# Gated cross-attention and two mixture-of-experts stages: the second stage's shared experts woven into the cross-attention, and ring numbers read at another place

## The chip, the cores and the metric

One NeuronCore of a Trainium2 chip runs the whole program in one launch. The metric is the device time in microseconds. Three runs of the kernel before gave 1206.42, 1208.92 and 1210.02 us; their median, 1208.92 us, is the time before. One more execution was profiled: it took 1207.77 us, of which the instructions span 1205.9 us.

## What is computed

2048 tokens (4 batches of 512) of 256 numbers go through four residual steps.

```python
x = x + tanh(g_xattn[0]) * windowed_attention(layernorm(x), ctx)       # 16 heads, window 64
x = x + tanh(g_ffn[0])   * moe0(layernorm(x))   # 32 experts of 128, top 8 in 4 of 8 groups, 1 shared expert of 128
x = x + tanh(g_xattn[1]) * bidaf(layernorm(x), ctx)
x = x + tanh(g_ffn[1])   * moe1(layernorm(x))   # 8 experts of 256, top 2 by softmax + bias, shared experts of 512 hidden

# bidaf, per batch (hc = normalised x, hq = ctx)
Sim = (hc@w1)[:,:,None] + (hq@w2)[:,None,:] + einsum('bid,bjd->bij', hc*w3, hq) + b
hq_hat = softmax(Sim, 2) @ hq
hc_bar = softmax(max(Sim, 2), 1) @ hc
out = concat([hc, hq_hat, hc*hq_hat, hc*hc_bar]) @ W_qv + b_qv
# moe1
scores = softmax(xt @ gate_w.T); idx = top_k(scores + gate_bias, 2); w = scores[idx]
y = sum_e w_e * (silu(xt@w1[e].T) * (xt@w3[e].T)) @ w2[e].T
z = silu(xt@sw1.T) * (xt@sw3.T) @ sw2.T
moe1 = y + z
```

## The kernel before

Five engines run programs written out by hand and meet at semaphores: TensorE (`pe`, shown as PE), ScalarE (`act`), VectorE (`dve`), GpSimd (`pool`) and SyncE (`sp`), which issues most loads. The residual `x` stays in on-chip memory as 16 tiles of 128 tokens. The order of work on each engine is the order of its code; nothing is scheduled automatically.

The program has five parts. First the windowed attention. Then the front of expert stage 0 (logits, routing, shared expert) and its sparse part: every (token, expert) choice has a slot, slots are cut into blocks of 128 that belong to one expert each, 159 blocks. Then the cross-attention, one iteration per batch (`tensor_a1`, `scalar_a1`, `vector_a1`). Then the front of expert stage 1 (`moe_tensor` and its fellows with `L == 1`) and its sparse part, 39 blocks, each with two halves of the expert's 256 hidden numbers. At the end the rows are gathered back and added.

The front of stage 1 treats the shared experts as 4 units of 128 hidden numbers and goes over unit and batch, v = 0 to 15. Inputs, weights and hidden values are split into a high and a low fp32r part (`xh`, `xl`, `wh`, `wl`, `hidh`, `hidl`), and each product is made of three: `gate_up` has 12 products of 512 columns per v, `down` 12 of 256 columns. The logits are 8 products of 512 columns per batch, turned by token afterwards. VectorE does the routing between those units: `first`, softmax, sort, mark, `ranked`, one-hot tables (`hots`, two buffers), index lists (`indices`).

In the cross-attention an iteration has on TensorE: `transposes` of the normalised input, `scores` (four products pairs into two banks, each waiting for VectorE's maximum and ScalarE's exp), `probs_transposed`, `attended`, `context_bar`, `output`. VectorE adds the gathered rows of stage 0 for the next batch in the middle of it (`y_pair_added`), takes the residual of the last batch, and normalises.

In the sparse parts (`sparse_tensor`) a step k has: `slots_transposed` of block i+2, `gate_up(k)`, `hidden_transposed(k - 1)`, `down(k - 2)`. The expert's weights lie in a ring of four, and the ring number of block i is read by TensorE's queue from a table in memory (`value_load`) at the head of the block, ahead of everything else of it; in stage 1 a second number is read there, the count of loads that must have landed.

## Time and profile before

| | us |
|---|---|
| median of three runs | 1208.92 |
| profiled execution | 1207.77 |
| its span | 1205.9 |
| PE busy | 919.2 (76%) |
| DVE busy | 733.9 (61%) |
| POOL busy | 531.6 (44%) |
| ACT busy | 442.2 (37%) |

By the trace the stretches are: sparse part of stage 0 from 377 to 658 us, cross-attention from 717.7 us (its second, third and fourth iteration begin at 763.1, 809.0 and 854.5, and the last product ends at 899.2), front of stage 1 until 1010.4, its sparse part until 1154, and the gathering of rows until the end. Matmuls overlap in the records: of a chain of products, the time from one start to the next tells more than the duration. A plain fp32 product appears as two records, an fp32r product or a transposition as one.

### The profile page before, as it was taken

Reading aid. Unit: us, or ns where it says so; the run is one execution under the profiler, and the core shown is the slowest. Engines: PE = TensorE matmul, PEld = TensorE weight load, DVE = VectorE, ACT = ScalarE, POOL = GpSimd, SP = SyncE. Lnnn points to the kernel's source line nnn. Section 1 sums busy time; section 2 is a strip of 40 time slices with the busy share of each in tenths; the row PEclk is TensorE's granted clock in tenths of the full one; section 3 lists DMA queues with packets and bytes.
Section 4 is the critical chain, followed back from the end, with each engine's and each line's share of the span. In section 5 each row is a group of like instructions: output and inputs, shape, how many; then the busy total and the mean of one; then the engine's idle time right before and its main releaser. Section 6 shows DMA issues by size and latency. Waiting matters only on the chain. (4 is left out here: it accounts for less than half of the span.)

```text
span 1205.9 us, 20553 instructions
## 1 busy us (share of the span) xinstructions
PE 919.2 (76%) x5501; PEld 693.9 (58%) x5501; DVE 733.9 (61%) x2093; ACT 442.2 (37%) x1048; POOL 531.6 (44%) x584
## 2 busy tenths in 40 slices
PE   3478888865577999999998019889898968999920
PEld 3467777753334777777776005455566856677610
DVE  6769999996654865555554255787744765433322
ACT  5559888943132333333333002202214241222200
POOL 7246656542004655555551777786002204222045
PEclk9679999988656999999999558987999989999965
DMA  8930000022002676666666534333014001335234
GB/s 248 216 72 2 0 0 0 1 67 70 1 0 66 210 208 193 201 205 206 186 170 128 196 98 128 113 105 88 1 42 133 2 1 57 102 86 152 83 101 130
DMA packets 65690, 122.62 MB, mean 102 GB/s; under 512 B 10497, under 2 KB 41474, under 8 KB 65474
## 3 DMA queue, kind: packets, MB, share of 16 engines
q0 software_dynamic: 17184, 46.95, 15.1%
q1 hardware_dynamic: 21474, 48.62, 13.8%
q10 hardware_dynamic: 26944, 25.96, 6.2%
q8 instruction: 45, 0.74, 0.2%
q14 instruction: 43, 0.35, 0.1%
HBM read 80.33 MB, written 32.24 MB: 93 GB/s over the span
## 5 line engine op out<-in xcount | busy, mean ns | idle before, releaser
L1278 POOL DMA_INDIRECT xg<-token_rows,gather_idx x198 | 188.1, 950 | 278.9 <-PE bank L944 182.7
L955 PE MATMUL bank<-sw,xgt 128*128 x948 | 255.0, 392 | 1.0 <-DVE shid L1208 0.9
L1294 POOL DMA_INDIRECT yg<-slot_rows,slot_of x160 | 170.1, 1063 | 111.7 <-DMA slot_rows<-ysb 63.5
L955 PEld LDWEIGHTS bank<-sw,xgt 128*128 128x128 f32 x948 | 166.2, 192 | 22.7 <-issue 2.6
L1075 ACT ACTIVATE ssil<-bank 128x128 f32<-128x128 f32 x237 | 65.7, 277 | 243.3 <-PE bank L955 243.3
L970 PE MATMUL bank<-sw,sht 128*128 x474 | 141.8, 381 | 0.0
L1202 DVE COPY xgt<-bank 128x256 f32<-128x256 f32 x198 | 83.8, 424 | 93.4 <-PE bank L944 91.1
L1215 DVE COPY sht<-bank 128x128 f32<-128x128 f32 x237 | 69.1, 292 | 117.3 <-PE bank L963 117.0
L548 ACT ACTIVATE prob<-bank,nmax 128x256 f32<-128x256 f32 x256 | 111.4, 510 | 7.1 <-DVE nmax L612 7.1
L1309 DVE SCALAR_TENSOR_TENSOR x<-yg,gate_of,x 128x256 f32<-128x256 f32 x160 | 65.8, 479 | 78.3 <-DMA yg<-slot_rows,slot_of 78.3
L430 PE MATMUL bank<-consts,prob 128*128 128x128 f32 x512 | 84.0, 289 | 33.5 <-DVE ptl L620 31.2
L612 DVE TENSOR_REDUCE nmax<-bank 128x2 f32<-128x512 f32 x128 | 87.7, 686 | 17.6 <-PE bank L417 17.1
L1082 ACT ACTIVATE ysb<-bank 128x256 f32<-128x256 f32 x198 | 75.9, 383 | 54.3 <-PE bank L970 54.3
L944 PE MATMUL bank<-consts,xg 128*128 128x128 f32 x396 | 79.1, 283 | 21.0 <-issue 10.1
L538 ACT ACTIVATE pth<-bank 128x512 f16<-128x512 f32 x128 | 80.0, 625 | 33.8 <-PE bank L430 33.5
L620 DVE TENSOR_TENSOR ptl<-bank,pth 128x512 f16<-128x512 f32 x128 | 87.2, 681 | 0.9 <-ACT pth L538 0.8
L944 PEld LDWEIGHTS bank<-consts,xg 128*128 128x128 f32 x396 | 48.1, 142 | 66.2 <-issue 51.4
L430 PEld LDWEIGHTS bank<-consts,prob 128*128 128x128 f32 x512 | 57.9, 146 | 48.5 <-ACT prob L548 26.7
L970 PEld LDWEIGHTS bank<-sw,sht 128*128 128x128 f32 x474 | 71.6, 191 | 18.1 <-issue 0.6
L417 PE MATMUL bank<-kst,qm 128*128 (+1 forms) x256 | 78.7, 391 | 0.0
L664 POOL TENSOR_TENSOR qm<-qst,consts 128x512 fp32r<-128x512 f32 x64 | 67.6, 1086 | 21.5 <-ACT qst L480 21.5
L881 PE MATMUL bank<-hot_hi,hot_tok 128*128 128x159 f16 (+1 forms) x160 | 43.6, 427 | 35.0 <-ACT hot_tok L1035 34.5
(211 smaller groups left out, 1688.1 us busy)
## 6 DMA issues: line engine op xcount, KB each, us to landing
slot_rows<-ysb ACTq DMA_DIRECT2D x98, 256.0 KB, 3.1
sw<-in_w SPq DMA_DIRECT2D x48, 384.0 KB
kst<-khl SPq DMA_DIRECT2D x32, 224.0 KB, 5.4
token_rows<-xn SPq DMA_DIRECT2D x8, 512.0 KB, 4.9
xg<-token_rows,gather_idx POOLq DMA_INDIRECT x198, 3.3
yg<-slot_rows,slot_of POOLq DMA_INDIRECT x160, 2.8
x<-in_x SPq DMA_DIRECT2D x4, 512.0 KB, 5.7
craw<-in_ctxt SPq DMA_DIRECT2D x4, 512.0 KB, 6.5
```

The costliest lines, as they stand in the source:

```text
L417: mm = pe.matmul(sp[:, hh * WIN:(hh + 1) * WIN], qm[:, par, hh, k, :], ks, start=False, stop=True, skip_group_check=True)
L430: mm = pe.transpose(bank[2 + (k + 1) % 2][:, hh * WIN + kb * P:hh * WIN + kb * P + P], prob[:, (k + 1) % 4, hh, kb * P:(kb + 1) * P], ident)
L538: nc.scalar.activation(pth[:, (k + 1) % 4], bank[2 + (k + 1) % 2][:, :].rearrange("p (a b) -> p a b", a=2), ACT.Copy).then_inc(s_pth, 1)
L548: e = nc.scalar.activation(prob[:, k % 4, hh, :], s_bank(k, par)[:, hh * WIN:(hh + 1) * WIN], ACT.Exp, bias=nmax[:, k % 4, hh:hh + 1])
L612: nc.vector.tensor_reduce(nmax[:, k % 4, :], s_bank(k, par)[:, :].rearrange("p (a b) -> p a b", a=2), AX_X, ALU.max, negate=True).then_inc ...
L620: nc.vector.tensor_tensor(ptl[:, k % 4], bank[2 + k % 2][:, :].rearrange("p (a b) -> p a b", a=2), pth[:, k % 4], ALU.subtract).then_inc(s ...
L944: mm = pe.transpose(bank[i % 2][:, c * P:(c + 1) * P], xg[:, (first + i) % XG_RING, c * P:(c + 1) * P], ident)
L955: mm = pe.matmul(bank[2 + k % 2][:, 0:2 * FF], xgt[:, i % 3, c * P:(c + 1) * P], w[:, :, c, :], start=(c == 0), stop=(c == CH - 1))
L970: pe.matmul(bank[6 + i % 2][:, 0:DIM], sht[:, k % 2, :], sw[:, bass.ds(slot[i] + u, 1), 2 * CH * FF:WCOLS], start=(u == 0), stop=(u == hal ...
L1202: nc.vector.tensor_copy(xgt[:, i % 3, :], bank[i % 2][:, 0:CH * P]).then_inc(s_xtl, 1)
L1278: nc.gpsimd.indirect_dma_start(xg[:, (first + i) % XG_RING, 0:ROW[L]], None, rows[L], bass.IndirectOffsetOnAxis(gather_idx[:, i:i + 1], 0) ...
L1294: nc.gpsimd.indirect_dma_start(yg[:, t % Y_TILES, j, :], None, ybuf[L], bass.IndirectOffsetOnAxis(slot_of[:, t, j:j + 1], 0)).then_inc(s_y ...
```

## The change

The front of stage 1 is taken apart. Its logits and shared experts are computed in plain fp32 instead of in three fp32r products, from one buffer of the turned input (`xt1`), one of all shared weights (`wsh1`) and one of hidden values (`hid1`), and they are put into the cross-attention: in iteration b the work of batch b-1 (and the down products of b-2). What is left after the last iteration is the work of the last batch and the routing. VectorE's row terms now come behind the four maxima, and the normalising of batch b-1 is done in one piece ahead of them. The one-hot tables have four buffers instead of two in both stages. TensorE reads the ring numbers of block i+1 behind the gate products of block i instead of at the head of block i+1.

```diff
+HOTS = 4
-                if t >= 2:
-                    dve.wait_ge(m.hotf, m.n["hotf"] + t - 1)
+                if t >= HOTS:
+                    dve.wait_ge(m.hotf, m.n["hotf"] + t - HOTS + 1)
...
+            def block_numbers(i):
+                slot[i] = pe.value_load(wslot[0:1, i:i + 1], min_val=0, max_val=W_RING - halves)
+                if L == 1:
+                    loads[i] = pe.value_load(needed[0:1, i:i + 1], min_val=16, max_val=16 * (E0 + 2 * E1))
+            block_numbers(0)
             slots_transposed(0)
             slots_transposed(1)
             for k in range(blocks * halves):
                 i = k // halves
                 if k % halves == 0:
-                    slot[i] = pe.value_load(wslot[0:1, i:i + 1], min_val=0, max_val=W_RING - halves)
                     if L == 1:
-                        pe.wait_ge(s_sw, pe.value_load(needed[0:1, i:i + 1], min_val=16, max_val=16 * (E0 + 2 * E1)))
+                        pe.wait_ge(s_sw, loads[i])
                     if i + 2 < blocks:
                         slots_transposed(i + 2)
                 gate_up(k)
+                if k % halves == 0 and i + 1 < blocks:
+                    block_numbers(i + 1)
                 if k >= 1:
                     hidden_transposed(k - 1)
...
+            def logits(b):
+                pe.wait_ge(m.xh, n1["xh"] + 2 * b + 2)
+                for j in range(TPB):
+                    for c in range(CH):
+                        mm = pe.matmul(bank[3][:, j * E1:(j + 1) * E1], xt1[:, c, j * P:(j + 1) * P], rraw[:, c, 0:E1],
+                                       start=(c == 0), stop=(c == CH - 1))
+                mm.then_inc(m.lg, 1)
+            def shared_gate_up(b, u):
+                v = SH1 * b + u
+                if v == 0:
+                    pe.wait_ge(m.wload, 16)
+                else:
+                    pe.wait_ge(m.h, n1["h"] + v)
+                if u == 0:
+                    pe.wait_ge(A["p"], 4 * min(b + 2, BATCH))
+                for half, ready in ((0, m.gate), (1, m.up)):
+                    for c in range(CH):
+                        w = slice((CH * half + c) * FF, (CH * half + c + 1) * FF)
+                        mm = pe.matmul(bank[half][:, :], wsh1[:, u, w], xt1[:, c, :], start=(c == 0), stop=(c == CH - 1))
+                    mm.then_inc(ready, 1)
...
             for b in range(BATCH):
                 transposes(b)
+                if b >= 2:
+                    shared_down(b - 2)
                 scores(b)
+                if b:
+                    inputs_turned(b - 1)
+                    logits(b - 1)
+                    shared_gate_up(b - 1, 0)
                 probs_transposed(b)
                 maxima_transposed(b)
                 attended(b)
+                if b:
+                    shared_gate_up(b - 1, 1)
                 context_bar(b)
+                if b:
+                    shared_gate_up(b - 1, 2)
+                output(b, (0,))
+                if b:
+                    shared_gate_up(b - 1, 3)
+                output(b, (2,))
+            b = BATCH - 1
+            shared_down(b - 1)
+            inputs_turned(b)
+            logits(b)
+            shared_gate_up(b, 0)
+            shared_gate_up(b, 1)
+            ranks(pe, 1, m)
+            shared_gate_up(b, 2)
+            table(pe, 1, m, range(0, 8))
+            shared_gate_up(b, 3)
+            table(pe, 1, m, range(8, TILES))
+            expert_row(pe, 1, m)
+            shared_down(b)
...
+            def shared_silu(b, u):
+                act.wait_ge(m.gate, m.n["gate"] + SH1 * b + u + 1)
+                if b:
+                    act.wait_ge(m.y, m.n["y"] + b)
+                nc.scalar.activation(hid1[:, u, :], bank[0][:, :], ACT.Silu).then_inc(m.sil, 1)
...
+                if b == 1:
+                    sp.dma_start(wsh1[:, :, :], w1_in[0:SH1].rearrange("u p c -> p u c")).then_inc(m.wload, 16)
+                if b >= 2:
+                    rows_stored(sp, 1, m, b - 2)
```

TensorE in the sparse part of stage 1, one block. L982 and L984 read the ring number and the load count, L944 transposes slots, L955 is gate and up, L963 turns the hidden values, L970 is down; ISA rows work out addresses. Before:

```order
L982 TENSOR_LOAD wslot
L982 ISA x2
L984 TENSOR_LOAD needed
L984 ISA x2
L944 MATMUL bank<-consts,xg 128x128 x2
L955 ISA
L955 MATMUL bank<-sw,xgt 128x256
L955 ISA
L955 MATMUL bank<-sw,xgt 128x256
L963 MATMUL bank<-consts,shid 128x128
```

The same block after, where L930 is the transposition of slots, L941 gate and up, L966 and L968 the reads, L949 the turning of hidden values, L956 down:

```order
L930 MATMUL bank<-consts,xg 128x128 x2
L941 ISA
L941 MATMUL bank<-sw,xgt 128x256
L941 ISA
L941 MATMUL bank<-sw,xgt 128x256
L966 TENSOR_LOAD wslot
L966 ISA x2
L968 TENSOR_LOAD needed
L968 ISA x2
L949 MATMUL bank<-consts,shid 128x128
L956 ISA
L956 MATMUL bank<-sw,sht 128x256
```

The reads have moved from ahead of the slots' transposition to between the gate and up products and the turning of hidden values.

TensorE in the third iteration of the cross-attention, from its first transposition to the attended product, before (L1589 `transposes`, L1600 `scores`, L1612 `probs_transposed`, L1633 `attended`):

```order
L1589 MATMUL bank<-consts,xn 128x128 x8
L1600 MATMUL bank<-craw,aenc 128x512 x8
L1612 MATMUL bank<-consts,prob 128x128 x16
L1618 MATMUL bank<-consts,mx 1x128
L1633 MATMUL bank<-p1t,traw 128x512 x4
```

And after (L1627 `shared_down`, L1590 `inputs_turned`, L1601 `logits`, L1617 `shared_gate_up`):

```order
L1503 MATMUL bank<-consts,xn 128x128 x8
L1627 MATMUL bank<-wsh,hid 128x256 x16
L1516 MATMUL bank<-craw,aenc 128x512 x8
L1590 MATMUL bank<-consts,xn 128x128 x8
L1601 MATMUL bank<-rraw,xt 128x8 x8
L1617 MATMUL bank<-xt,wsh 128x512 x4
L1528 MATMUL bank<-consts,prob 128x128 x16
L1534 MATMUL bank<-consts,mx 1x128
L1551 MATMUL bank<-p1t,traw 128x512 x4
```

Sixteen down products stand behind the first transpositions, and a transposition, the logits and one unit's gate and up stand behind the scores; three more units follow later in the iteration.

## Rows read from the trace of the kernel before

**Rows 1.** Busy time of each engine by stretch; last columns: TensorE's clock, DMA share, GB/s.

```profile
763.10:809.00 45.90, 38.63 (x134) 23.35 (x134) 36.52 (x118) 7.84 (x18) 36.08 (x32) 0.89 0.39 115
809.00:854.50 45.50, 41.22 (x133) 25.09 (x133) 36.05 (x118) 8.05 (x18) 23.64 (x23) 0.81 0.24 70
854.50:899.20 44.70, 38.60 (x149) 25.11 (x150) 21.30 (x67) 10.44 (x23) 0.00 (x0) 0.92 0.00 0
899.20:1010.40 111.20, 89.84 (x514) 70.96 (x512) 73.25 (x255) 38.01 (x64) 25.18 (x20) 0.95 0.18 57
377.00:658.00 281.00, 277.33 (x1431) 217.04 (x1431) 157.38 (x501) 104.40 (x317) 148.83 (x157) 0.99 0.66 187
```

**Rows 2.** TensorE in order of time, one block of stage 1's sparse part.

```profile
1037.54 0.41 PE L944 MATMUL bank<-consts,xg 128*128 128x128 f32 x2 [0.32 <-issue]
1038.85 0.60 PE L970 MATMUL bank<-sw,sht 128*128 x2
1039.28 1.03 PE L955 MATMUL bank<-sw,xgt 128*128 x4
1040.25 0.60 PE L970 MATMUL bank<-sw,sht 128*128 x2
1041.12 0.41 PE L944 MATMUL bank<-consts,xg 128*128 128x128 f32 x2 [0.27 <-issue]
```

**Rows 3.** Reads of ring numbers by TensorE's queue, whole program: duration in ns min/median/max.

```profile
L982 PEldq TENSOR_LOAD <-wslot x198: 296/303/857, 378.3 to 1148.0; - x198
```

**Rows 4.** The two reads of the block of Rows 2, and VectorE's hidden values.

```profile
L982 PEldq TENSOR_LOAD <-wslot x1: 306/306/306, 1039.7 to 1039.7; - x1
L984 PEldq SEQ_ASSERT  x1: 18/18/18, 1040.9 to 1040.9; - x1
1039.26 0.28 DVE L1208 TENSOR_TENSOR shid<-ssil,bank 128x128 f32<-128x128 f32 x1
```

**Rows 5.** Stage 0's sparse part: the slots' transpositions of 148 blocks, then two in order of time.

```profile
L944 PE MATMUL bank<-consts,xg x296: 272/273/391, 384.1 to 640.0; 128*128 128x128 f32 x148
...
387.46 0.38 PE L944 MATMUL bank<-consts,xg 128*128 128x128 f32 x2
389.09 0.38 PE L944 MATMUL bank<-consts,xg 128*128 128x128 f32 x2
```

**Rows 6.** TensorE in order of time, third iteration of the cross-attention.

```profile
808.97 1.09 PE L1589 MATMUL bank<-consts,xn 128*128 128x128 f32 x8 [2.75 <-DVE xn L762]
811.92 10.17 PE L1600 MATMUL bank<-craw,aenc 128*128 128x512 f32 x16 [1.86 <-issue]
824.45 3.65 PE L1612 MATMUL bank<-consts,prob 128*128 128x128 f32 x16 [2.36 <-DVE prob L1744]
831.91 3.70 PE L1633 MATMUL bank<-p1t,traw 128*128 128x512 f32 x8
835.45 0.28 PE L1639 MATMUL bank<-ebs,ones 128*128 128x1 f32 x2
835.59 1.93 PE L1642 MATMUL bank<-eb,xn 128*128 128x1 f32 x16
```

**Rows 7.** TensorE, front of stage 1: one unit's gate and up, one unit's down, by starts.

```profile
912.46 0.40 PE L838 MATMUL bank<-xh,wh 128*128 128x512 f32 x1
915.23 1.03 PE L778 MATMUL bank<-consts,xn 128*128 128x128 f32 x8
932.48 0.28 PE L855 MATMUL bank<-wh,hidh 128*128 128x256 f32 x1
933.91 0.40 PE L838 MATMUL bank<-xh,wh 128*128 128x512 f32 x1
```

**Rows 8.** VectorE, front of stage 1: ranking and the hidden values behind it.

```profile
958.25 0.28 DVE L1392 TENSOR_TENSOR more<-bank,thresholds 128x128 f32<-128x128 f32 x1
963.27 0.69 DVE L1130 TENSOR_TENSOR hid<-sil,bank 128x512 f32<-128x512 f32 x1
```

**Rows 9.** TensorE, one-hot products of a pair of tiles in stage 0.

```profile
323.91 4.78 PE L881 MATMUL bank<-hot_hi,hot_tok 128*128 128x159 f16 x16 [0.42 <-ACT hot_tok L1035]
```

More of the change, by code:

```diff
@@ L304, in __init__ @@
                 self.rs = sem(f"route_step{n}")
-                self.wload = [sem(f"w_loaded_{i}_{n}") for i in range(2)]
+                self.wload = sem(f"w_loaded_{n}")
                 self.rload = own["rload"]
@@ L1058, in moe_scalar @@
[L1058 to L1066 removed]
+            hidden_hi(2)
+            act.wait_ge(m.lgl, 1)
+            nc.scalar.activation(sc[:, :, :], lg[:, :, :], ACT.Sigmoid).then_inc(m.ra, 1)
@@ L1068, in sparse_scalar @@
+            silu(3)
+            hidden_hi(3)
+            hots_by_token(act, 0, m, range(TILES))
         def sparse_scalar(act, L, m):
@@ L1159, in moe_vector @@
             first()
-            if L == 0:
-                for part in routing:
-                    part()
-                hidden(3)
-                add(0)
-                ranked()
-                weights()
-                add(1)
-                hots(range(0, 4))
-                add(2)
-                hots(range(4, 8))
-                add(3)
-                hots(range(8, TILES))
-                indices()
-            else:
-                add(0)
-                add(1)
-                parts = {4: routing[0:1], 5: routing[1:2], 6: routing[2:3], 8: (ranked,), 9: (weights,)}
-                for v in range(3, 4 * nb):
-                    hidden(v)
-                    if v == 8:
-                        dve.wait_ge(m.y, m.n["y"] + 8)
-                    if v >= 8:
-                        hidden_lo(v)
-                    add(v - 1)
-                    for part in parts.get(v, ()):
-                        part()
-                    if 9 <= v < 13:
-                        hots(range(4 * (v - 9), 4 * (v - 9) + 4))
-                    if v == 13:
-                        indices()
-                add(4 * nb - 1)
+            for part in routing:
+                part()
+            hidden(3)
+            add(0)
+            ranked()
+            weights()
+            add(1)
+            hots(range(0, 4))
+            add(2)
+            hots(range(4, 8))
+            add(3)
+            hots(range(8, TILES))
+            indices()
         def sparse_vector(dve, L, m):
@@ L1342, in sparse_sync @@
         def sparse_sync(sp, L, m, w_in):
+            for v in range(W_RING):
+                expert_load(sp, L, w_in, v)
             sp.wait_ge(m.exp, m.n["exp"] + 1)
@@ L1644, in context_bar, with output @@
                 mm.then_inc(A["hb"], 1)
-            def output(b):
-                for j0 in (0, 2):
+            def output(b, halves):
+                for j0 in halves:
                     for g, f in ((1, hq), (2, prod), (0, enc)):
@@ L1712, in scalar_a1, with vector_a1 @@
                 attended_copied(b)
-                if b == BATCH - 1:
-                    x_high(act, moe[1], 0)
-                    x_high(act, moe[1], 1)
-        def vector_a1(dve, root):
+                if b:
+                    for u in range(1, SH1):
+                        shared_silu(b - 1, u)
+            b = BATCH - 1
+            inputs_copied(b)
+            shared_silu(b, 0)
+            act.wait_ge(m.rs, 2)
+            nc.scalar.activation(rep[:, :, 0:E1], msc[:, :, 0:E1], ACT.Exp).then_inc(m.ra, 1)
+            shared_silu(b, 1)
+            shared_silu(b, 2)
+            hots_by_token(act, 1, m, range(0, 8))
+            shared_silu(b, 3)
+            hots_by_token(act, 1, m, range(8, TILES))
+        def vector_a1(dve, root, m, first, routing, tables):
+            ranked, weights, hots, indices = tables
             def row_terms(b):
@@ L1835, in vector_a1 @@
                     ln_norm(dve, 2, b + 1, A["xn"])
-                else:
-                    x_low(dve, moe[1], 0)
-                    x_low(dve, moe[1], 1)
-            residual(BATCH - 1)
+                if b:
+                    shared_hidden(b - 1, 3)
+            b = BATCH - 1
+            residual(b)
+            attended_normalised(b)
+            shared_added(b - 1)
+            logits_taken(b)
+            dve.wait_ge(m.ltc, m.n["ltc"] + BATCH)
+            first()
+            shared_hidden(b, 0)
+            for part in routing:
+                part()
+            shared_hidden(b, 1)
+            ranked()
+            shared_hidden(b, 2)
+            hots(range(0, 8))
+            shared_hidden(b, 3)
+            hots(range(8, TILES))
+            indices()
+            weights()
+            shared_added(b)
         def pool_a1(pool):
```

494 lines of the change are left out of this document (231 added, 263 removed).

## The prediction

> **What bounds the kernel now.** I read the busy shares first: TensorE is busy 76% of the span, so it is the engine to follow, but no stage can be costed by a mean. So I cut the span into stretches [rows 1]. In stage 0's sparse part (377 to 658) TensorE is busy nearly throughout, at full clock; in the cross-attention it is busy some 85% and its granted clock is 0.81 to 0.92; in the front of stage 1 it is busy 90 of 111 us. Then I read each stretch in order of time on TensorE, for what stands between one start and the next.
>
> In stage 1's sparse part a block lasts from 1037.54 to 1041.12, 3.58 us. The second half's gate, up, turning and down take from 1039.28 to 1040.25 plus 0.43, that is 1.40 us, and 0.43 is the down pair (1038.85 to 1039.28). The next block should start at 1040.68 and starts at 1041.12, "issue" before it: 0.44 us lost, and 0.1 more in the first products after the stall [rows 2]. Free of that a block is 2 x 1.41 for the halves and 0.22 for the slots' transposition, 3.04 us. "Issue" means that TensorE's own queue was late. Why: reading one number takes 0.30 us, with 0.15 and 0.02 for its two companions and the steps between 0.64 in all [rows 3], and there are two. They start at 1039.7 and the last ends at 1040.9 [rows 4].
>
> **Part one: ring numbers.** What sets the start of the reads decides. VectorE's hidden values of the first half are ready at 1039.26 + 0.28 = 1039.54, and the reads start 0.17 us later [rows 4]. So they did not wait for a full array queue: the queue was held by the wait of `hidden_transposed`, then issued the down pair, then the reads. At 1039.7 there was 1040.68 - 1039.7 = 0.98 us of products in hand, against 1.43 us for reads and the step behind them: the 0.44. In the new order the reads stand ahead of that wait. The queue passes the wait at 1039.54, pushes down, slots' transposition, gate and up (about 0.75 us, by the steps of 0.13 us between the hidden values' end and the reads) and starts reading some 0.9 us behind the wait; the array then still holds down, transpositions and four records of gate and up, 0.43 + 0.22 + 0.86 = 1.5 us, more than 1.43. So the reads should be hidden. 38 blocks x 0.54 = 20.5 us. What is late next: the two weight loads of an expert, with blocks of 3.04 instead of 3.6; I leave 1 us for that. Gain 19.5 us. Bounds: 0 if the products in hand are no more than before, 21 if all goes.
>
> In stage 0 there is one read per block. 148 blocks take from 384.1 to 640.0, 255.9 / 147 = 1.740 us each, while an undisturbed one takes 389.09 - 387.46 = 1.63 [rows 5]. The difference, 0.11 x 157 = 17 us, I ascribe to reads, since they are short at the median and long, to 0.857, in others [rows 3]: a long one outlasts the 0.98 us. Behind the gate products even a long read (1.2 us with its companions) has cover. I take 15; bounds 0 and 17.
>
> The Trainium skill ("TensorE: Matmul & The Clock Gate", architectural detail, engine queue depths) gives TensorE a queue of 64 entries. By that rule 1.5 us of products, some nine records, can be in hand and the gain stands; were the queue about as deep as the five records seen in hand at a read, the gain would be nil. The trace shows only the five, since there the wait held the queue and not its depth, so the rule moves my chance and not the sum.
>
> **Part two: the woven shared experts.** Plain fp32 costs more of TensorE: four products of 512 columns are eight records, by the attended product 3.54 us per eight [rows 6], against 12 fp32r products in 915.23 - 912.46 = 2.77. Down is four products of 256 columns per tile quartet, 4 x 0.43 = 1.73 (a pair of records is 0.43 [rows 2]) against 1.43 [rows 7]. Over 16 units: 16 x (5.27 - 4.20) = 17 us more work. It pays only if it fills waits and if the routing, now alone behind the loop, is short.
>
> An iteration: added are the turning 0.9, a wait for ScalarE's two copies 1.8 (a transposition's end to `scores` is 1.86 by such a chain [rows 6]), logits 1.9 (16 records with few columns, [rows 6]), four gate and up 14.2 and one down 6.9 (not in the second iteration). Third iteration: 45.6 + 25.7, less the waits that now have work in them: 1.86 ahead of the scores, 10.17 - 7.1 = 3.1 in them, 2.36 ahead of the probabilities [rows 6]: 64.0. Fourth: 44.7 + 25.7 less 1.9, 1.5, 2.4 and less the 16 transpositions of stage 1 that stood in it, 3.8: 60.8. Second: 45.9 + 18.8, less 2.36 and less the 2.75 of waiting for the next input, which TensorE no longer meets; plus 3.3, since normalising (statistics 1.85, root 2.6, norm 1.4) now stands ahead of the first maximum and the row terms (2.3) behind: 62.9. The first is fed by gathered rows as before. Start 763.1, so the last output ends at 763.1 + 187.7 = 950.8 instead of 899.2: 51.6 us later.
>
> Behind it a chain through VectorE. Counted from the last output: residual 1.1, normalising 5.9, turning and copies 2.0, logits 1.9, maximum and difference 0.9, ScalarE's exp behind one Silu and a table load 3.0, hidden unit 0.7, softmax, sort and mark 1.25 + 1.4 + 2.8, unit 0.7 and TensorE's ranks 3.4, `ranked` 5.0 (958.25 to 963.27 [rows 8]), unit 0.7, eight one-hots 4.9 with their lag, gate and up of the last unit 3.5 and its hidden values 0.7, eight more 3.9, list 0.6, down 6.9 and its addition 1.7. Sum 53. Before, the same distance is 1010.4 - 899.2 = 111.2 [rows 1]. So the sparse part starts at 950.8 + 53 = 1003.8. ScalarE's table loads between Exp and Silu lie beside TensorE's products; were they not hidden, nine of 1.3 us. The index list is ready some 9 us before the end of that chain and the first gather lands about 4.9 later, so in time for the first block.
>
> The clock: the iterations have 0.89, 0.81 and 0.92 of full clock [rows 1], though TensorE waited only some 7 us in each. The one-column products of `context_bar` stay, and logits and their wait are a new thin place. With TensorE the bound, each us at the lower level costs half a us that was partly waiting before. I add 3.5: start at 1007.3, 3 us earlier than before. Bounds: the skipped waits give nothing and the clock falls as often as in the third iteration (+15), or it holds (-11).
>
> **Part three: four one-hot buffers.** TensorE stood 0.42 us between pairs of tiles in stage 0, 4.77 us each [rows 9], five such gaps: 2 us. It is TensorE's low-clock product time that sets the rest. Other moves (one weight buffer in stage 0, stores of rows inside the loop, one 1.5 MB load of shared weights while gathers run, issue-bound then) I cost at nothing: the load has about 90 us until its first use; were it to delay the gathers before the first iteration, 3 us.
>
> **Sum.** -15 - 2 - 3 - 19.5 = -39.5. On the profiled execution 1207.8 - 39.5 = 1168.3; the median of the runs lies 1.1 us higher: 1169.4, I say 1169.
>
> **Rivals.**
> Ahead of the reads there is no more in hand than before (slower). Place: `hidden_transposed`, now behind the reads. Price: the 0.44 us of 39 blocks and the stalls of about 55 blocks of stage 0 stay, and behind them stands one turning of 0.11 us instead of two transpositions before address work and a pair of records: about 0.12 us more per stall, 94 x 0.12 = 11. With parts two and three: 1208.9 - 5 + 11 = 1215. It decides if under about six records can be in hand. For it: no row shows more than five at a read. Against it: rows 4 show the queue held by a wait.
> The woven loop is dearer by its clock: part two costs +12 instead of -3: 1184. For it 0.81 in the third iteration; against it 281 us of fp32 products at 0.99.
> The loop gains more, -14: the denser loop keeps full clock: 1158.
> The reads pay half, as more of them are long or weight loads show: 1186.
> Part two does worse still, +40, if about half of it runs at the low level (the work is some 200 us at full clock): no change or slower.
>
> **How the numbers follow.** Forecast 0.62 (own range 1157 to 1183); clock or half the reads 0.16; holding clock 0.09; uncovered reads 0.09, two thirds of it slower; low clock throughout 0.04. A measurement tells 0.3% (3.6 us). Faster 0.87, same 0.05, slower 0.08. Range: 1153 to 1200, leaving the 1215 case and the tails out.
>
> **What would show it.** Starts of the slots' transposition in stage 1's sparse part 3.0 to 3.1 us apart, without "issue", and 1.63 to 1.65 in stage 0; else part one is wrong. Iterations two to four of 61 to 66 us with hardly a wait on TensorE; the sparse part starting 50 to 58 us behind the last output. If it starts later than 1015 (by the old count, less what stage 0 gained), part two failed.

## The result and the profile after

Four runs of the changed kernel gave 1168.08, 1170.15, 1174.03 and 1175.38 us, median 1172.09, against 1209.45 for the kernel before in the same four rounds: ratio 0.970, 95% interval 0.968 to 0.972. Forecast was 1169. The profiled execution took 1170.15 us and spans 1168.3 us, 37.6 less than before.

To see where they went I cut both spans at the same five places. The cuts are starts of TensorE's instructions in the two traces (the first transposition of slots of a stage, the first transposition of the cross-attention, the last product):

| us | before | after | difference | forecast |
|---|---|---|---|---|
| until stage 0's sparse part | 377.8 | 374.0 | -3.8 | -2 |
| sparse part 0 and gathering, to the cross-attention | 339.9 | 321.1 | -18.8 | -15 |
| cross-attention and front of stage 1 | 292.7 | 288.9 | -3.8 | -3 |
| stage 1's sparse part, to the last product | 143.4 | 132.1 | -11.3 | -19.5 |
| gathering and adding of rows | 52.1 | 52.2 | 0 | 0 |

The sum is nearly the forecast one, but its terms are not: stage 1's sparse part gained 8.2 us less than forecast, and the three others together 6.4 us more. The rows that answer to [rows 1], with the same columns (busy us and count of TensorE, its weight loads, VectorE, ScalarE and GpSimd; then granted clock, DMA share, GB/s). The fourth iteration ends at 927.4 and what follows it, the last batch's work and the routing, is called the tail:

```profile
374.00:636.00 262.00, 261.26 (x1431) 219.62 (x1431) 156.95 (x501) 104.46 (x317) 148.46 (x157) 0.99 0.70 200
...
695.10:742.20 47.10, 41.04 (x134) 25.46 (x135) 29.77 (x89) 9.44 (x19) 36.71 (x35) 0.81 0.41 120
742.20:804.60 62.40, 53.37 (x190) 30.73 (x189) 39.29 (x123) 14.94 (x27) 41.78 (x41) 0.95 0.37 110
804.60:865.20 60.60, 58.43 (x222) 36.12 (x221) 40.55 (x127) 16.33 (x28) 11.40 (x12) 0.97 0.13 37
865.20:927.40 62.20, 60.09 (x223) 37.56 (x221) 23.55 (x72) 16.33 (x28) 0.00 (x0) 0.95 0.03 9
927.40:984.00 56.60, 44.08 (x186) 27.48 (x184) 31.09 (x174) 13.34 (x25) 7.56 (x8) 0.85 0.18 56
```

Stage 0's 1431 products take 262 us at 99.7% busy: nothing is left there but the products. (The busy share alone would not have shown the gain: before, the same products were busy for 277.33 of 281 us, 98.7%.) The second to fourth iterations are 60.6 to 62.4 us long and 86, 96 and 97% busy; the granted clock, 0.81 to 0.92 in the old ones, is 0.95 to 0.97 in them.

Now a block of stage 1's sparse part, TensorE in order of time, the counterpart of [rows 2]:

```profile
1029.06 0.27 PE L949 MATMUL bank<-consts,shid 128*128 128x128 f32 x1
1029.17 0.60 PE L956 MATMUL bank<-sw,sht 128*128 x2
1029.60 0.38 PE L930 MATMUL bank<-consts,xg 128*128 128x128 f32 x2
1029.82 1.03 PE L941 MATMUL bank<-sw,xgt 128*128 x4
1030.68 0.27 PE L949 MATMUL bank<-consts,shid 128*128 128x128 f32 x1
...
1032.64 0.27 PE L930 MATMUL bank<-consts,xg 128*128 128x128 f32 x1
```

and its two reads on TensorE's queue, the counterpart of [rows 4]; behind them VectorE's hidden values of the half before:

```profile
L966 PEldq TENSOR_LOAD <-wslot x1: 300/300/300, 1029.0 to 1029.0; - x1
...
L968 PEldq SEQ_ASSERT  x1: 18/18/18, 1030.3 to 1030.3; - x1
```

```profile
1029.57 0.28 DVE L1149 TENSOR_TENSOR shid<-ssil,bank 128x128 f32<-128x128 f32 x1
```

From 1029.60 to 1032.64 are 3.04 us, with no "issue". The reads start at 1029.0, before the hidden values are ready (1029.85), and end at 1030.3, 0.4 us before the turning is due at 1030.68. When they start, the array has in hand, that is issued by the queue and not yet run, the turning at 1029.06, the down pair, two transpositions and four records of gate and up: nine products, 1.68 us (1030.68 - 1029.0), against five in [rows 2, 4], counted in the same way. That was the point on which my rival "uncovered reads" hung; it is out. The Trainium skill ("TensorE: Matmul & The Clock Gate", architectural detail, engine queue depths) allows far more, 64; the trace agrees as far as nine, and no run here shows more.

So why only 11.3 us and not 19.5? The waits of TensorE in that stretch answer (engine, operation, what for: us, times, longest):

```profile
PE bank L930 <- issue: 3.1, 1, 3.1
PE bank L949 <- issue: 3.0, 5, 0.7
PE bank L930 <- DMA sw<-in_w: 2.3, 4, 1.0
```

The first is the start of the part. The other two belong together, as TensorE in order of time shows where a new expert begins:

```profile
1062.89 0.44 PE L930 MATMUL bank<-consts,xg 128*128 128x128 f32 x2 [0.16 <-DMA sw<-in_w]
1063.16 1.06 PE L941 MATMUL bank<-sw,xgt 128*128 x4
1064.95 0.30 PE L949 MATMUL bank<-consts,shid 128*128 128x128 f32 x1 [0.73 <-issue]
```

The weights are late by a few tenths (0.16 before the transpositions; up to 1.0 at other experts), and in that wait the queue has pushed nothing ahead. The reads behind the gate products then find only those in hand and show again with 0.73 us. Behind the first two, blocks are 3.03 to 3.29 us apart until 1048; from there on, with an expert every three blocks, two of each three last 3.4 to 4.2 us and the third 3.03 to 3.05. 16 blocks from 1048.1 to 1105.9 take 57.7 us; at 3.10, the mean of the 18 ahead of them, 49.7. That is 8.0 us where I had left 1, so 7 of the 8.2 us that are missing; the mean of 3.10 in place of 3.04 ahead of them accounts for about one more. Why the weights are late stands in the loads themselves (SyncE's queue, all twelve of the part):

```profile
L1255 SPq DMA_DIRECT2D sw<-in_w x12: 327/328/333, 1014.2 to 1092.4; - x12
...
DMA to landing us min/median/max: 2.9/3.2/3.8
```

Each half of an expert lands 3.2 us after its issue, and the second is only issued when the first has landed (1056.6 and 1059.7, for instance): 6.4 us from a free ring to a complete expert, against two blocks of 3.04.

### The profile page after: what moved, and what is told of

It is laid out like the page before. It is cut to its first block, busy times and chain, and to the rows that moved or that the text cites. A ratio compares the mean times of both kernels' runs of the same rounds, so it can differ in the third digit from the quotient of the medians.

```text
span 1168.3 us, 20181 instructions
## 1 busy us (share of the span) xinstructions
PE 905.8 (78%) x5388; PEld 687.2 (59%) x5389; DVE 699.6 (60%) x2031; ACT 439.2 (38%) x1033; POOL 507.0 (43%) x572
## 4 chain that ended last, share of the span: by engine, by line
PE 58%; DVE 18%; issue 7%; DMA 6%; POOL 4%; ACT 3%; SPq 1%; DVEq 0%; POOLq 0%; ACTq 0%
PE bank L941 17%; PE bank L956 8%; PE bank L1617 5%; PE bank L1578 4%; POOL yg L1224 4%; DVE ptl L625 4%; PE bank L930 4%; PE bank L823 3%; DVE nmax L617 3%; PE bank L1551 2%; DMA sw<-in_w 2%; PE bank L949 2%; PE bank L435 2%; PE bank L1516 2%; DMA yg<-slot_rows,slot_of 2%
## 5 line engine op out<-in xcount | busy, mean ns | idle before, releaser
L941 PE MATMUL bank<-sw,xgt 128*128 x948 | 246.2, 382 | 0.2 <-issue 0.2
L1224 POOL DMA_INDIRECT yg<-slot_rows,slot_of x160 | 163.6, 1023 | 116.9 <-DMA slot_rows<-ysb 60.6
L941 PEld LDWEIGHTS bank<-sw,xgt 128*128 128x128 f32 x948 | 166.0, 192 | 15.5 <-issue 1.0
L956 PE MATMUL bank<-sw,sht 128*128 x474 | 143.7, 385 | 0.0
L930 PE MATMUL bank<-consts,xg 128*128 128x128 f32 x396 | 77.0, 277 | 11.3 <-DMA xg<-token_rows,gather_idx 5.3
L956 PEld LDWEIGHTS bank<-sw,sht 128*128 128x128 f32 x474 | 71.4, 191 | 19.5 <-issue 1.4
L930 PEld LDWEIGHTS bank<-consts,xg 128*128 128x128 f32 x396 | 55.5, 143 | 34.0 <-DMA xg<-token_rows,gather_idx 6.3
L1617 PE MATMUL bank<-xt,wsh 128*128 128x512 f32 x128 | 68.1, 682 | 0.8 <-DVE hid L1823 0.8
```

What stands on the lines that cost most here:

```text
L930: mm = pe.transpose(bank[i % 2][:, c * P:(c + 1) * P], xg[:, (first + i) % XG_RING, c * P:(c + 1) * P], ident)
L941: mm = pe.matmul(bank[2 + k % 2][:, 0:2 * FF], xgt[:, i % 3, c * P:(c + 1) * P], w[:, :, c, :], start=(c == 0), stop=(c == CH - 1))
L956: pe.matmul(bank[6 + i % 2][:, 0:DIM], sht[:, k % 2, :], sw[:, bass.ds(slot[i] + u, 1), 2 * CH * FF:WCOLS], start=(u == 0), stop=(u == hal ...
L1224: nc.gpsimd.indirect_dma_start(yg[:, t % Y_TILES, j, :], None, ybuf[L], bass.IndirectOffsetOnAxis(slot_of[:, t, j:j + 1], 0)).then_inc(s_y ...
L1617: mm = pe.matmul(bank[half][:, :], wsh1[:, u, w], xt1[:, c, :], start=(c == 0), stop=(c == CH - 1))
```

## The experiments

The twelve runs were made in three groups (e1 to e4, e5 to e8, e9 to e12), each beside the kernel before, whose medians were 1211.7, 1208.8 and 1208.3 us. So kernels of different groups are compared by their ratios. The last four columns are us of one profiled execution each, cut at the same places as above; "middle" is the cross-attention and the front of stage 1.

| | ratio to before | 95% interval | until 0 | sparse 0 | middle | sparse 1 |
|---|---|---|---|---|---|---|
| changed kernel, first and again | 0.970, 0.967 | 0.968-0.972, 0.965-0.969 | 374.0, 373.7 | 321.1, 322.4 | 288.9, 289.3 | 132.1, 132.5 |
| e1 reads at the head | 0.990 | 0.987-0.992 | 374.5 | 339.7 | 288.2 | 142.7 |
| e2 two one-hot buffers | 0.975 | 0.972-0.977 | 376.8 | 322.6 | 290.8 | 135.4 |
| e3 before, reads moved | 0.976 | 0.974-0.979 | 378.0 | 323.2 | 292.8 | 133.1 |
| e4 paired loads | 0.963 | 0.960-0.965 | 373.0 | 322.9 | 284.9 | 123.6 |
| e6 woven front alone | 0.998 | 0.996-0.999 | 378.0 | 340.6 | 289.1 | 144.6 |
| e7 reads doubled | 1.105 | 1.102-1.108 | 375.3 | 445.9 | 289.1 | 172.4 |
| e8 reads before gate and up | 0.994 | 0.992-0.995 | 374.4 | 337.5 | 284.7 | 146.7 |
| e9 before, paired loads | 1.000 | 0.998-1.003 | 377.8 | 339.2 | 293.0 | 143.6 |
| e10 e4 and early one-hots | 0.963 | 0.960-0.966 | 373.6 | 321.1 | 289.2 | 122.5 |
| e11 reads behind the turning | 0.994 | 0.992-0.996 | 375.3 | 331.0 | 287.4 | 151.9 |
| e12 e10 with split reads | 0.960 | 0.957-0.963 | 375.4 | 322.8 | 288.2 | 122.0 |

**e1: the reads back.**

```diff
-            block_numbers(0)
             slots_transposed(0)
...
                 if k % halves == 0:
+                    block_numbers(i)
                     if L == 1:
                         pe.wait_ge(s_sw, loads[i])
...
-                if k % halves == 0 and i + 1 < blocks:
-                    block_numbers(i + 1)
```

> The changed kernel with the reads of ring numbers put back at the head of each block, in both stages; front and one-hot buffers stay as changed. If the reads are what the sparse parts gained (my theory), stage 0's blocks go back from 1.64 to 1.74-1.76 us each and its part lasts 16 to 19 us longer, stage 1's blocks go back to 3.60 us and its part lasts 11 us longer (not 19.5, since 8 us of the stalls had covered late expert weights): 1172 + 27 to 30 = 1199 to 1202 us. If the sparse parts gained from something else that changed with them (single weight buffers, other timing of the loads), block times stay within 0.02 us of the changed kernel's and the time stays near 1172.

1199.1 us. Stage 0's part is 18.6 longer, stage 1's 10.6, the rest within 0.7 us. The 0.44 are back, too:

```profile
1032.63 0.41 PE L930 MATMUL bank<-consts,xg 128*128 128x128 f32 x2 [0.27 <-issue]
...
1036.23 0.41 PE L930 MATMUL bank<-consts,xg 128*128 128x128 f32 x2 [0.29 <-issue]
```

The reads are all of the gain in the sparse parts (339.7 and 142.7 us here, 339.9 and 143.4 in the kernel before). The tail is 1.2 us shorter, 55.5 against 56.6: the first two transpositions of slots no longer stand behind block 0's reads.

**e2: two one-hot buffers** (`HOTS = 2`).

> The changed kernel with two one-hot buffers in place of four. Stage 0's sparse part began 3.8 us earlier in the changed kernel, where I had put 2. If the buffers are all of it, it begins at 377.8 again and the time is 1172 + 3.8 = 1176, plus up to 1 us for the pairs of tiles in stage 1's tail. If most of those 3.8 us came from the single weight buffer and the other order of ScalarE's copies, it begins within 1 us of 374 and the time is 1172 to 1173.

1180.2 us. The sparse part of stage 0 begins at 376.8, and in e6, also with two buffers and the woven front, at 378.0, as before; the nine profiles with four buffers have 373.0 to 375.4. So about 3 us at the start are the buffers', and the single weight buffer gave nothing that shows. The whole is 6 to 9 us slower than the changed kernel by the ratios, more than the 4 to 5 I expected. The rest is in the tail of stage 1's front. TensorE's waits for one-hot tables there, in the changed kernel and in e2:

```profile
PE bank L823 <- ACT hot_tok L997: 5.0, 2, 3.2
```

```profile
PE bank L823 <- ACT hot_tok L997: 9.5, 8, 3.2
```

Six waits of 0.75 us are added, one between the products of a pair of tiles and the next pair's, and the tail lasts 62.2 us against 56.6. I had allowed 1 us for that. The middle as a whole is only 1.9 us longer because the fourth iteration took 58.9 us in this execution instead of 62.2; profiles with four buffers have both values too (see the clock, below). Stage 1's sparse part is 3.3 us longer, with weights late by 3.9 us in place of 2.3; e5, the changed kernel again, has 3.0, so part of this is scatter.

**e3: only the reads, in the kernel before.** `block_numbers` as in the change, nothing else.

> The kernel before with nothing changed but the place of the reads: behind the gate and up products of a block's first half, one block ahead. If the reads act alone and apart from the front (theory): stage 0 -16 to -19, stage 1 -11 (with expert weights late in its last third, as in the changed kernel), 1209.4 - 28.5 = 1181 us (1178 to 1184). If the sparse gain needs the woven front (other landing times of weights and rows), less: 1190 or more. If late weights are a matter of the woven front, stage 1 gains the full 19.5 here: 1172 to 1174.

1181.8 us. -16.7 in stage 0 and -10.3 in stage 1: the reads act alone, and the late weights come with them, not with the woven front.

**e5: the changed kernel again.**

> The changed kernel once more, unaltered, as the measure for the kernels that run beside it on this chip. 1172 us (1168 to 1176) and a ratio of 0.970 to the kernel before.

1169.95 us, ratio 0.967. The two ratios of the same kernel, 0.970 and 0.967, show what a comparison between groups can tell: 0.3%.

**e6: the woven front alone** (e1's edit and `HOTS = 2`).

> The changed kernel with the reads back at the head of each block and with two one-hot buffers: of the change only the woven front of stage 1 is left (with what comes with it, one weight buffer in stage 0). If the front is worth what the traces say (loop 50.8 us longer, the way from the last output to the sparse part 54.6 shorter), the time is before minus 3 to 5 us. Two buffers in its shorter routing may cost 1 to 2 of it. If the clock in the loop or the tail decides against it in most runs, it lies within 1.5 us of before or above.

1206.0 us, -2.9 (-4.7 to -1.1). The profile has 289.1 for the middle against 292.7. The eleven profiles with this front have 284.7 to 290.8, the three with the old one 292.7 to 293.0: a gain of 2 to 8 us from one execution to the next, 4.7 in the mean. With two buffers, as here, the tail is 60.9 us long; e1, which differs from e6 only in having four, has 55.5. So the front by itself gained about 3 us, and four buffers shortened its tail by some 5.5 more, a gain for which the forecast had no term of its own.

**e4: the two halves' loads together.**

```diff
-            if v:
+            if v and (L == 0 or v % 2 == 0):
                 sp.wait_ge(s_sw, 16 * (E0 * L + v))
```

> The changed kernel, where in stage 1 the loads of an expert's two halves are issued together: the second no longer waits for the first to land. In the changed kernel stage 1's blocks last 3.03 to 3.15 us until 1048 and then, with an expert per three blocks, 4.2, 4.0 and 3.03 in turn: 8 us lost to late weights (waits of 0.2 to 1.0 us) and to the reads behind each such wait, which find nothing in hand (0.7). If the second half is late because its load starts when the first has landed (theory), the blocks go to 3.1 throughout and the time is 1172 - 6 to 8 = 1164 to 1166. If the two transfers share the same bandwidth, so that both land when the second did before, the time stays at 1172 within 1.5.

1165.0 us; stage 1's part 123.6 us, 8.5 less. The whole time is 5 to 9 us shorter than the changed kernel's, by the two ratios of the latter. TensorE's waits in it, whole:

```profile
PE bank L930 <- issue: 3.1, 1, 3.1
PE bank L930 <- DVE xgt L1143: 0.5, 1, 0.5
```

The weight waits are gone, and with them the five stalls of the reads behind them. Bandwidth was no obstacle.

**e9: the same edit in the kernel before.**

> The kernel before, with the loads of an expert's two halves issued together and nothing else. In the changed kernel the same edit gave 7 us. If the reads' stalls of 0.44 us per block had covered the late weights (theory), here it gives 0 to 2 us: 1207 to 1209, blocks of 3.60 as before. If weights bound stage 1 in the kernel before too, it gives 5 us or more.

Ratio 1.000, stage 1's part 143.6 us as before. Here the block's start waits 0.26 to 0.43 us whatever is named:

```profile
1102.21 0.41 PE L944 MATMUL bank<-consts,xg 128*128 128x128 f32 x2 [0.26 <-issue]
...
1105.81 0.41 PE L944 MATMUL bank<-consts,xg 128*128 128x128 f32 x2 [0.29 <-DMA sw<-in_w]
```

The stall by the reads had given every expert's weights enough time: two blocks of 3.6 us are 7.2, more than the 6.4 of two landings. An edit worth 8.5 us of stage 1 in one kernel is worth nothing in the other.

**e7: each read twice.**

```diff
                 if k % halves == 0 and i + 1 < blocks:
                     block_numbers(i + 1)
+                    pe.value_load(wslot[0:1, i + 1:i + 2], min_val=0, max_val=W_RING - halves)
+                    if L == 1:
+                        pe.value_load(needed[0:1, i + 1:i + 2], min_val=16, max_val=16 * (E0 + 2 * E1))
```

> The changed kernel with each read of ring numbers done twice, at the same place: 4 reads per block in stage 1 (2.86 us with their steps), 2 in stage 0 (1.28). If what covers them is the products in hand since the wait for the hidden values, 1.55 us (theory): stage 0's blocks stay at 1.63 to 1.66 (a long read costs more now), stage 1's last 3.10 + 1.3 = 4.4 us and its part about 170 us instead of 132, less some us of late weights covered: 1172 + 40 = 1212 (1203 to 1218). If much more could be in hand than those 1.55 us, blocks of stage 1 stay near 3.1 and the time below 1180. If only about five records could be, the changed kernel would already stall, which it does not.

1337.8 us, not 1212. Stage 1 came as expected (blocks of 4.2 to 4.6 us as a rule, 4.32 at the median; its part 172.4 us). Stage 0 did not: blocks went from 1.63 to 2.30 at the median and 2.42 in the mean, 125 us for reads that I had thought covered. The array in order of time, then the queue's reads (L983 is the added one; min/median/max ns, starts):

```profile
450.82 1.03 PE L941 MATMUL bank<-sw,xgt 128*128 x4
452.36 0.30 PE L949 MATMUL bank<-consts,shid 128*128 128x128 f32 x1 [0.51 <-issue]
...
454.53 0.30 PE L949 MATMUL bank<-consts,shid 128*128 128x128 f32 x1 [0.16 <-issue]
```

```profile
L966 PEldq TENSOR_LOAD <-wslot x1: 308/308/308, 450.6 to 450.6; - x1
L983 PEldq TENSOR_LOAD <-wslot x1: 671/671/671, 451.2 to 451.2; - x1
...
L966 PEldq TENSOR_LOAD <-wslot x1: 305/305/305, 453.1 to 453.1; - x1
```

From read to read are 2.5 us, 0.37 of them because one read was long. The two reads with companions take 451.2 - 450.6 twice, 1.3 us; the other 0.85 is the queue's own work for a block's products. The products in hand can bridge one late moment, but not a queue that has more work per block than the array: 0.85 + 1.3 = 2.15 against 1.63, and more where a read is long. With single reads it is 0.85 + 0.65 = 1.5 against 1.63. I had counted cover only and not throughput; the changed kernel has 0.1 us of margin per block by this sum.

**e8: reads ahead of gate and up.**

```diff
+                if k % halves == 0 and i + 2 < blocks:
+                    block_numbers(i + 1)
                 gate_up(k)
-                if k % halves == 0 and i + 1 < blocks:
+                if k % halves == 0 and i + 2 == blocks:
                     block_numbers(i + 1)
```

> The changed kernel with the reads one step earlier: behind the slots' transpositions, ahead of the gate and up products of the same half. By the theory the cover is what was pushed since the wait for the hidden values: down 0.43 and transpositions 0.22 and what was left of the half before (0.5 us), without the four records of gate and up (0.86): about 1.1 us against reads of 1.43 with their step, so a stall of 0.3 to 0.4 us per block in stage 1 (3.4 to 3.5 us, part +9 us where weights aren't late, less 4 of late weights covered) and of long reads in stage 0 (+5 to +12 us): 1172 + 10 to 17 = 1182 to 1189. If anything ahead of the hidden values' wait is as good as any other place (rival), it stays at 1172 to 1175.

1201.9 us: the whole gain of the reads is gone (+16.4 us in stage 0, +14.6 in stage 1 against the changed kernel), two to three times the loss expected. Blocks of stage 1 last 3.61 us, as with reads at the head:

```profile
1032.74 0.38 PE L930 MATMUL bank<-consts,xg 128*128 128x128 f32 x2
1033.40 1.12 PE L941 MATMUL bank<-sw,xgt 128*128 x4 [0.27 <-issue]
```

The stall only moved from ahead of the transpositions to behind them. The likely reason (no run separates it): I had counted the transpositions as additional cover; but gate and up come from the same queue, and between the wait and their issue stand the same reads in either order.

**e11: reads behind the turning.**

```diff
                 gate_up(k)
-                if k % halves == 0 and i + 1 < blocks:
-                    block_numbers(i + 1)
                 if k >= 1:
                     hidden_transposed(k - 1)
+                if k % halves == 0 and i + 1 < blocks:
+                    block_numbers(i + 1)
```

> The changed kernel with the reads one step later: behind the turning of the hidden values, ahead of down. The wait for the hidden values then stands ahead of the reads again. Theory, corrected by the doubled and the earlier reads (what counts is which wait the reads stand behind, and that all products behind them come from the same queue): from that wait the array has about 0.9 us in hand, against 0.65 to 1.2 in stage 0 and 1.43 in stage 1. Blocks of 3.5 to 3.6 us in stage 1, of 1.70 to 1.78 in stage 0, 1190 to 1203 us. If it is enough that the gate and up products stand ahead of the reads (my reasoning in the prediction), it stays at 1172 to 1176.

1201.4 us. Stage 1 is the worst of all single reads, 3.82 us a block, stage 0 better than expected, 1.67. There few reads were long: 9 of stage 0's 159 took over 0.35 us, against 65 in the kernel before and 58 in the changed one. The length of a read thus depends on where in the block it stands; what makes it long stays open. TensorE and VectorE in order of time:

```profile
1034.15 0.27 PE L949 MATMUL bank<-consts,shid 128*128 128x128 f32 x1
1035.64 0.69 PE L956 MATMUL bank<-sw,sht 128*128 x2 [1.21 <-DVE sht L1156]
```

```profile
1034.46 0.29 DVE L1156 COPY sht<-bank 128x128 f32<-128x128 f32 x1 [0.55 <-PE bank L949]
```

The row blames VectorE's copy, yet that copy ended at 1034.75, 0.9 us before the products started. The queue was still reading:

```profile
L968 PEldq TENSOR_LOAD <-needed x1: 1034/1034/1034, 1034.0 to 1034.0; - x1
...
L968 PEldq SEQ_ASSERT  x1: 18/18/18, 1035.3 to 1035.3; - x1
```

(This read was one of four long ones of 39; the median is 0.305, and the blocks with two short reads stall as well, mostly by 0.45 to 0.55.) Here one sees that the name behind the arrow is only the latest semaphore and that the wait is the queue's. The four places (head of the block, ahead of gate and up, behind them, behind the turning) give ratios of 0.990, 0.994, 0.967 to 0.970 and 0.994: only the one ahead of the wait and behind the largest batch of products pays.

**e10: early one-hots.** On e4; VectorE's and ScalarE's work for all sixteen tiles' one-hots stands ahead of the last unit's hidden values (VectorE's side shown; ScalarE's copies move in the same way).

```diff
-            hots(range(0, 8))
+            hots(range(0, TILES))
             shared_hidden(b, 3)
-            hots(range(8, TILES))
```

> The changed kernel with paired expert loads, and in the last part of stage 1's front all sixteen one-hots (VectorE's and ScalarE's part) ahead of the last unit's hidden values, where eight stood behind them. TensorE waited 1.76 us for the latter eight ahead of their products and VectorE stood idle for 7 us before. If that wait is on the path: 2 to 3 us less than paired loads alone (0.9627 of before), 1162, the sparse part starting 54 to 55 us behind the last output in place of 56.6. If ScalarE's Silu of the last unit now stands behind its eight copies and is late, the wait only moves to the last down: within 1 us of paired loads alone.

1163.4 us, no gain over e4. Not ScalarE's Silu but the buffers decide: with four, only tiles 8 to 11 can be made early, the others wait for the products of these, behind the unit.

```profile
966.69 0.77 PE L823 MATMUL bank<-hot_hi,hot_tok 128*128 128x39 f16 x8
968.18 1.62 PE L823 MATMUL bank<-hot_hi,hot_tok 128*128 128x39 f16 x8 [0.72 <-ACT hot_tok L997]
971.25 0.19 PE L830 MATMUL bank<-started,ones 8*1 8x39 bf16 x1 [1.45 <-DVE started L1370]
```

The 1.76 us of waiting became 0.72 and 1.45.

**e12: split reads.** On e10, the slot's number is read behind the first half's gate and up, the needed count behind the second half's.

```diff
-                if k % halves == 0 and i + 1 < blocks:
-                    block_numbers(i + 1)
+                if i + 1 < blocks:
+                    block_numbers(i + 1, (k % halves,))
...
```

> As the kernel with paired loads and early one-hots, and in stage 1 the two reads of a block stand apart: the slot's number behind the first half's gate and up products, the needed count behind the second half's. The queue then has 0.7 us of reads against 0.86 of products each time. If the blocks of 3.10 to 3.16 us that alternate with 3.03 are the queue coming late, all go to 3.04 and it gains 38 x 0.07 = 2.5 us. If they are something else (a gather's landing, VectorE's copies), the same time within 1 us. If the second read costs where it stood free, slower by up to 5.

1161.5 us, ratio 0.960. Blocks of stage 1 are 3.034 us at the median, where e10 has 3.08, so the alternating 3.10 to 3.16 were the queue coming late. Behind its first three blocks the part is 2.0 us shorter than e10's (103.2 us against 105.2), near the 2.5 expected. The part as a whole gains only 0.5, since here the first three took 8.8 us against 7.0, at a granted clock of 0.65 (986.4 to 995.2 us) against 1.00 (983.9 to 991.0 in e10's trace).

The times don't separate e4, e10 and e12. e12 is the fastest kernel that ran, 4.0% ahead of before (3.7 to 4.3). Of its gain over the changed kernel, 0.7 to 1.0% by the ratios, the paired loads of e4 have 0.5 to 0.7%.

## Why the prediction was right, and where it was not

The time was right to 3 us. The mechanisms were right, but that the sum came so near is luck: 8.2 us missing in one term were made good by 6.4 us too much in three others.

*Reads in stage 1, -19.5 forecast, -11.3 measured.* The stall went, block by block, as worked out (3.04 us, [rows 2] against the rows above). The step that failed is "what is late next: I leave 1 us for that". It was 8.0 us, and it is the serial loading of an expert's halves, which e4 removes (with it stage 1's part gained 19.8 us over before, 143.4 to 123.6). The rows to see it were there: an expert needs two loads one after the other, and a block was to shrink by 0.54 us; I never set the sum of two landings against the time until the expert is due. What I also missed is that each such wait empties the queue, so that the hidden reads show again behind it: of the loss, 3.0 us are of that kind.

*Reads in stage 0, -15 forecast, -18.8 measured,* 16.7 and 18.6 by e3 and e1. I had found 17 by [rows 5] and taken less out of caution. The trace bears out that it is the long reads: in the kernel before 65 of stage 0's 159 reads took 0.41 to 0.86 us, the block with such a read was longer than 1.64 us in 55 of 64 cases, the one behind it lasted 1.73 at the median, and of the 30 blocks with no such read in them or just before, 28 lasted 1.63. The mechanism had a hole nonetheless: with e7, cover by products in hand is not enough, the queue's work per block must be less than the array's.

*One-hot buffers, -2 forecast, -3.8 measured* in stage 0's front, 6 to 9 in the whole by e2. [rows 9] gave 0.42 us idle between products. A start is 0.59 us later for each such gap, as products of a chain overlap and the first after a pause does not; five of these are 3, and the first pair of tiles starts 0.6 earlier. The larger part, 5.5 us in stage 1's tail, was not in this term: the prediction counted the buffers' gain in stage 0 alone, and its 53 us for the tail hold the one-hots of four buffers (4.9 and 3.9 us) without a word on what two would cost there.

*The woven front, -3 forecast, -3.8 in the profile, -2.9 by e6* (which has two buffers). The sizes inside: iterations two to four 62.4, 60.6 and 62.2 us against 62.9, 64.0 and 60.8 worked out; the tail 56.6 against 53; the old front gone, 111.2. The second iteration was not free of waits, as I had said it would be (5.1 us ahead of its second pair of scores), but as long as worked out. A term put at nothing was the first iteration ("fed by gathered rows as before"): it lasts 47.1 us against 45.4 (46.5 to 48.8 in the eleven profiles with this front, 44.1 to 45.4 in the three with the old one). VectorE's row terms, 2.1 us, now stand between the last maximum and the last normalised probabilities, and TensorE waits for these, before and after:

```profile
733.07 1.09 PE L1612 MATMUL bank<-consts,prob 128*128 128x128 f32 x8 [2.38 <-DVE prob L1744]
```

```profile
712.32 3.32 PE L1528 MATMUL bank<-consts,prob 128*128 128x128 f32 x16 [4.42 <-DVE prob L1758]
```

I had charged that move to the second iteration only. The clock, for which 3.5 us were set aside, was better in the loop than before (0.95, 0.97 and 0.95 in its second to fourth iteration), but the rival that gave this case -14 had its size wrong. And it was low in two places. One is the tail (a stretch of it, then the down products in the loop and in the tail):

```profile
957.00:977.00 20.00, 16.70 (x56) 10.00 (x57) 8.59 (x42) 7.47 (x17) 3.34 (x4) 0.66 0.05 15
```

```profile
805.48 7.07 PE L1627 MATMUL bank<-wsh,hid 128*128 128x256 f32 x32
...
971.81 9.09 PE L1627 MATMUL bank<-wsh,hid 128*128 128x256 f32 x32
```

Twenty of its 56.6 us ran at 0.66 of full clock, a mixture of 1.2 and 2.4 GHz, and the last down takes 2 us more than the one in the loop. The other place is the fourth iteration, and only in some executions. The logits and the first gate and up in the changed kernel's profile, then the same rows in e4's:

```profile
883.02 3.12 PE L1601 MATMUL bank<-rraw,xt 128*128 128x8 f32 x16 [1.69 <-ACT xt L1699]
885.99 5.86 PE L1617 MATMUL bank<-xt,wsh 128*128 128x512 f32 x8
```

```profile
883.44 1.95 PE L1601 MATMUL bank<-rraw,xt 128*128 128x8 f32 x16 [1.70 <-ACT xt L1699]
885.25 3.68 PE L1617 MATMUL bank<-xt,wsh 128*128 128x512 f32 x8
```

From 885.2 to 895.2 the granted clock is 0.74, in e4 from 885.6 to 895.6 it is 1.00, for the same work behind the same wait of 1.7 us. Six of the eleven profiles with this front have the slow form and a fourth iteration of 62.2 us, four have the fast one and 58.9, one lies between (60.6). With the tail's length by the number of one-hot buffers this accounts for nearly all of the 6 us by which the middle varies. It also shows that a wait of TensorE alone doesn't decide whether the clock falls: of the tail's low stretch, which follows waits of 1.77 and 3.24 us, the cause is not shown either, and what decides in the fourth iteration stays open.

*Rivals.* Uncovered reads: refuted by the changed trace, with nine products in hand. A dearer loop: refuted, its clock rose (0.95 to 0.97 against 0.81 to 0.92), though in six of eleven executions its fourth iteration paid 3.3 us to the clock. Reads that pay half: nearly true of stage 1 (11.3 of 19.5), and by one of the reasons named there (weight loads show), but not of stage 0. Low clock in half of part two, +40: refuted, the middle got shorter in all eleven profiles.

## What to carry to other kernels

An instruction that holds an engine's queue cost nothing here where it stood behind a batch of issued work and ahead of the next wait, and where the queue's whole work per round was below the array's; one place earlier or later cost the whole gain. Before a stall is removed, ask what has been living off it: here each block's 0.44 us gave the weights time to land, and the same fix of the loads was worth nothing before and 8.5 us of that stage after. Put the landing times of a serial chain of loads beside the new, shorter period, not the old one. And when a part is costed with a resource it shares with another part, as the tail with its four buffers, take the resource away in a run before the gain is ascribed.

## What the runs showed of the hardware

Nine products were in hand of TensorE at once. A read of a number into its queue took 0.30 us as a rule and 0.4 to 0.86 in others (65 of 198 reads of slot numbers in the kernel before, 47 in the changed one, 4 with the reads behind the turning), up to 1.1 us in the experiments, with 0.35 for companions and steps. Both halves of an expert's weights in flight together landed in time for every expert, which one after the other they did not. Behind the same wait of 1.7 us and for the same products, the granted clock was 0.74 over 10 us in one execution and 1.00 in another, at a price of 3.3 us.
